# Gated cross-attention block: scores signalled by bank, and another order of the early vector and scalar work

## What is computed

```python
def reference(x, ctx, g_xattn, g_ffn, Wq, Wk, Wv, Wo, bo, w1, b1, w2, b2):
    def attention(y, context):                    # 8 heads of 64
        q, k, v = heads(y @ Wq), heads(context @ Wk), heads(context @ Wv)
        attn = softmax(einsum('bhnd,bhmd->bhnm', q, k) * 64 ** -0.5, axis=-1)
        return merge(einsum('bhnm,bhmd->bhnd', attn, v)) @ Wo + bo
    def ffn(y):                                   # 256 -> 1024 -> 256, 8-bit fixed point
        h = relu(fixed_quant(quantized_linear(y, w1, b1), 8, 4))
        return quantized_linear(h, w2, b2)
    x = x + tanh(g_xattn[0]) * attention(layernorm(x), ctx)
    return x + tanh(g_ffn[0]) * ffn(layernorm(x))
```

## Time and profile before

| | us |
|---|---|
| median of 3 runs | 120.61 |
| the runs | 119.7, 120.61, 376.62 |
| profiled execution | 120.01 |
| its span, first to last instruction | 118.2 |
| TensorE busy in the span | 111.8 (95%) |
| VectorE busy | 97.7 (83%) |
| GpSimd busy | 89.1 (75%) |
| ScalarE busy | 76.4 (65%) |

### The profile page before, as it was taken

One profiled execution on the slowest core, in us unless ns is written; L12 is line 12 of the kernel. 1 busy time (PEld: TensorE's weight loads), 2 busy tenths in 40 slices (PEclk: granted clock), 3 DMA queues, 4 the chain that ended last, 5 costly groups with the idle time before them and its releaser, 6 DMA issues.

```text
span 118.2 us, 2898 instructions
## 1 busy us (share of the span) xinstructions
PE 111.8 (95%) x1012; PEld 102.1 (86%) x1012; DVE 97.7 (83%) x223; ACT 76.4 (65%) x169; POOL 89.1 (75%) x161
## 2 busy tenths in 40 slices
PE   7979997899999999999999999999999999999990
PEld 2659976899798999988999999999999999897870
DVE  3029798999999999989999999999797979648981
ACT  4137766869688894998667575748483819448420
POOL 4003587698796989898989978996899999988720
PEclk9999999999999999999999999999999999999999
DMA  4989799300000000000010002000200020020204
GB/s 80 315 247 386 280 375 399 152 0 8 0 3 0 6 3 0 0 6 0 0 74 15 6 0 89 0 3 6 89 0 0 3 89 6 0 89 8 88 13 165
DMA packets 5328, 8.87 MB, mean 75 GB/s; under 512 B 1191, under 2 KB 2242, under 8 KB 5186
## 3 DMA queue, kind: packets, MB, share of 16 engines
q1 hardware_dynamic: 5082, 8.34, 20.1%
q10 hardware_dynamic: 232, 0.34, 0.9%
HBM read 6.59 MB, written 2.10 MB: 73 GB/s over the span
## 4 chain that ended last, share of the span: by engine, by line
PE 52%; POOL 21%; DVE 14%; DMA 5%; issue 3%; ACT 1%; SPq 1%; POOLq 0%; DVEq 0%; ACTq 0%
PE sc_ps L841 15%; PE of_ps L878 12%; PE h_ps L910 7%; DMA wq_sb<-in_L_xattn_Wq_dram 5%; POOL hid L362 5%; POOL x_sb L383 4%; PE of_ps L925 4%; POOL probs L300 4%; POOL rstd L310 3%; POOL yq L316 3%; DVE probs L614 3%; PE tr_ps L853 3%; DVE mx L609 3%; DVE den L621 2%; DVE pT L650 1%
## 5 line engine op out<-in xcount | busy, mean ns | idle before, releaser
L841 PE MATMUL sc_ps<-a_sb,xT 128*128 128x308 f32 x192 | 31.1, 311 | 0.7 <-DVE probs L614 0.7
L878 PE MATMUL of_ps<-u_sb,pT 128*128 128x256 f32 x240 | 30.9, 281 | 0.1
L878 PEld LDWEIGHTS of_ps<-u_sb,pT 128*128 128x128 f32 x240 | 29.5, 188 | 0.3 <-issue 0.3
L841 PEld LDWEIGHTS sc_ps<-a_sb,xT 128*128 128x128 f32 x192 | 27.4, 188 | 1.4 <-issue 1.2
L438 ACT ACTIVATE probs<-probs,rstd 128x616 f32<-128x616 f32 x16 | 13.1, 818 | 23.0 <-DVE probs L614 23.0
L481 ACT ACTIVATE hid_q<-h_ps,b1z 128x256 int8<-128x256 f32 x58 | 24.5, 494 | 3.6 <-PE h_ps L910 3.6
L300 POOL TENSOR_TENSOR probs<-probs,rden 128x616 f32<-128x616 f32 x16 | 19.5, 1221 | 1.9 <-DVE rden L624 1.9
L362 POOL CAST hid<-hid_q 128x512 bf16<-128x512 int8 x27 | 15.8, 611 | 2.0 <-ACT hid_q L481 2.0
L910 PE MATMUL h_ps<-x2T,w1T 128*128 128x256 bf16 x128 | 16.7, 274 | 0.0
L609 DVE TENSOR_REDUCE mx<-sc_ps 128x8 f32<-128x616 f32 x16 | 12.6, 787 | 2.8 <-PE sc_ps L841 2.7
L614 DVE TENSOR_TENSOR probs<-sc_ps,mx 128x616 f32<-128x616 f32 x16 | 12.8, 800 | 0.5
(11 more groups left out here) (124 smaller groups left out, 175.8 us busy)
## 6 DMA issues: line engine op xcount, KB each, us to landing
w_sb<-in_L_ffn_w_dram SPq DMA_DIRECT2D x2, 1024.0 KB, 10.9
out_dram<-x_sb SPq DMA_DIRECT2D x7, 256.0 KB, 2.5
x_sb<-in_x_dram SPq DMA_DIRECT2D x4, 256.0 KB, 8.0
x_sb<-in_x_dram SPq DMA_DIRECT2D x1, 1024.0 KB, 9.8
wq_sb<-in_L_xattn_Wq_dram SPq DMA_DIRECT2D x1, 512.0 KB, 5.8
wv_sb<-in_L_xattn_Wv_dram SPq DMA_DIRECT2D x1, 512.0 KB, 7.8
wo_sb<-in_L_xattn_Wo_dram SPq DMA_DIRECT2D x1, 512.0 KB, 8.6
wk_sb<-in_L_xattn_Wk_dram SPq DMA_DIRECT2D x1, 256.0 KB, 3.4
```

Source lines behind the costliest of these rows:

```text
L841: ins = nc.tensor.matmul(sc_ps[:, a, 0:HALF], xT[:, T % 2, p, c, :], a_sb[:, q, T // TB, c, HALF * a:HALF * a + HALF], start=first, stop=last)
L878: ins = nc.tensor.matmul(attn_ps, pT[:, T % 2, p, P * c:P * c + P], u_sb[:, q, MC * (T // TB) + c, :], start=first, stop=last)
```

## The change

TensorE makes the scores of bank 0 first, six matmuls, with a signal of their own, and then those of bank 1. The semaphores scores_ready, max_ready and centered count banks instead of tiles; the scores of bank a wait only for the subtraction of bank a of the tile before. center(T) takes the banks that it is to work on. Tiles 0 and 1 are centred one bank at a time, all others both at once as before. VectorE's prologue: tile 3's statistics go behind center(0), together with tile 4's; denominators(0) goes ahead of rowsT_low(2); tile 5's statistics go ahead of center(1); u_low(0, 0) goes between the two banks of center(1). In slot 0 VectorE runs probsT_low(0) ahead of denominators(1). ScalarE's prologue: exponentials(0) goes ahead of xT_copy(2), and minus_centred(3) behind it; in slot 0 pT_copy(0) and xT_copy(3) go ahead of exponentials(1). Nothing of GpSimd's or SyncE's changes.

```diff
--- before.py
+++ after.py
@@ -434,7 +434,7 @@
 
             def exponentials(T):
                 act.wait_ge(rstd1_ready, T + 1)
-                act.wait_ge(centered, T + 1)
+                act.wait_ge(centered, 2 * T + 2)
                 nc.scalar.activation(probs_v(T), probs_v(T), ACT.Exp, scale=rstd1[:, T:T + 1]).then_inc(exp_done, 1)
 
             def a_copy(n):
@@ -531,11 +531,11 @@
             act.wait_ge(v_psum, 1)
             nc.scalar.copy(values_of(0), values_psum(0)).then_inc(v01_ready, 1)
             minus_centred(2)
-            minus_centred(3)
             act.wait_ge(v_psum, 2)
             nc.scalar.copy(values_of(1), values_psum(1)).then_inc(v23_ready, 1)
+            exponentials(0)
             xT_copy(2)
-            exponentials(0)
+            minus_centred(3)
             u_copy(0, 0)
             u_copy(0, 1)
             u_copy_whole(0, 1)
@@ -545,10 +545,14 @@
             nc.scalar.activation(tg[:, :], g_sb[:, :], ACT.Tanh).then_inc(tg_ready, 1)
 
             for s in range(TILES):
+                if s == 0:
+                    pT_copy(0)
+                    xT_copy(3)
                 if live(s + 1):
                     exponentials(s + 1)
-                pT_copy(s)
-                if live(s + 3):
+                if s > 0:
+                    pT_copy(s)
+                if s > 0 and live(s + 3):
                     xT_copy(s + 3)
 
                 if s in (3, 4):
@@ -596,24 +600,33 @@
                 nc.vector.memset(pads[:, 0, 0:HEAD0], 1.0).then_inc(pad_set, 1)
 
             def stats_first(first, end):
-                dve.wait_ge(x_in[min(first, TB) // 2], 16)
                 for T in range(first, end):
+                    dve.wait_ge(x_in[min(T, TB) // 2], 16)
                     nc.vector.bn_stats(st1[:, T, :], x_sb[:, T, :]).then_inc(st1_done, 1)
                 for T in range(first, end):
                     dve.wait_ge(st1_done, T + 1)
                     nc.vector.bn_aggr(mv1[:, T, :], st1[:, T, :]).then_inc(mv1_ready, 1)
 
-            def center(T):
-                i = T % 2
-                dve.wait_ge(scores_ready, T + 1)
-                nc.vector.tensor_reduce(mx[:, i, :].rearrange("p (a h) -> p a h", a=2), sc_v, AX.X,
-                                        ALU.max).then_inc(max_ready, 1)
-                dve.wait_ge(max_ready, T + 1)
+            def maxima(T, banks):
+
+                i, h = T % 2, slice(H // 2 * banks[0], H // 2 * banks[-1] + H // 2)
+                dve.wait_ge(scores_ready, 2 * T + banks[-1] + 1)
+                nc.vector.tensor_reduce(mx[:, i, h].rearrange("p (a h) -> p a h", a=len(banks)),
+                                        sc_v[:, banks[0]:banks[-1] + 1, :, :], AX.X, ALU.max).then_inc(max_ready, len(banks))
+
+            def subtract_maxima(T, banks):
+                i, h = T % 2, slice(H // 2 * banks[0], H // 2 * banks[-1] + H // 2)
+                dve.wait_ge(max_ready, 2 * T + banks[-1] + 1)
                 if T >= 2:
                     dve.wait_ge(pT_psum, T - 1)
-                nc.vector.tensor_tensor(probs_v(T).rearrange("p (a h) m -> p a h m", a=2), sc_v,
-                                        mx[:, i, :].rearrange("p (a h) -> p a h", a=2).unsqueeze(3)
-                                        .to_broadcast([P, 2, H // 2, M]), ALU.subtract).then_inc(centered, 1)
+                nc.vector.tensor_tensor(probs_v(T)[:, h, :].rearrange("p (a h) m -> p a h m", a=len(banks)),
+                                        sc_v[:, banks[0]:banks[-1] + 1, :, :],
+                                        mx[:, i, h].rearrange("p (a h) -> p a h", a=len(banks)).unsqueeze(3)
+                                        .to_broadcast([P, len(banks), H // 2, M]), ALU.subtract).then_inc(centered, len(banks))
+
+            def center(T, banks=(0, 1)):
+                maxima(T, banks)
+                subtract_maxima(T, banks)
 
             def denominators(T):
                 i = T % 2
@@ -707,24 +720,29 @@
                                     of_ps[:, 0, :].rearrange("p (i n) -> p i n", i=2),
                                     xT[:, :, 0, :, :].rearrange("p i c n -> p i (c n)").bitcast(F32),
                                     ALU.subtract).then_inc(xT_ready, 2)
-            stats_first(2, 4)
-            center(0)
+            stats_first(2, 3)
+            center(0, (0,))
+            center(0, (1,))
+            stats_first(3, 5)
+            denominators(0)
             rowsT_low(2)
-            stats_first(4, 5)
-            denominators(0)
+            stats_first(5, 6)
+            center(1, (0,))
             u_low(0, 0)
-            center(1)
+            center(1, (1,))
             u_low(0, 2)
-            stats_first(5, 6)
             dve.wait_ge(tg_ready, 1)
 
             for s in range(TILES):
                 if live(s - 1):
                     residual(s - 1)
                     stats_second(s - 1)
+                if s == 0:
+                    probsT_low(0)
                 if live(s + 1):
                     denominators(s + 1)
-                probsT_low(s)
+                if s > 0:
+                    probsT_low(s)
                 if live(s + 3):
                     rowsT_low(s + 3)
                 if s == 4:
@@ -825,22 +843,23 @@
 
             def scores(T):
                 pe.wait_ge(xT_high, T + 1)
-                if T >= 1:
-                    pe.wait_ge(centered, T)
                 if T == TB:
                     pe.wait_ge(a1_high, DK)
                     pe.wait_ge(a1_low, DK)
-                for p, q in PARTS:
-                    if q == 1 and T == 0:
-                        pe.wait_ge(a_ready, len(a_units))
-                    if p == 1:
-                        pe.wait_ge(xT_ready, T + 1)
-                    for c in range(DK):
-                        for a in range(2):
+                for a in range(2):
+
+                    if T >= 1:
+                        pe.wait_ge(centered, 2 * T - 1 + a)
+                    for p, q in PARTS:
+                        if q == 1 and T == 0:
+                            pe.wait_ge(a_ready, len(a_units))
+                        if p == 1:
+                            pe.wait_ge(xT_ready, T + 1)
+                        for c in range(DK):
                             first, last = (c, p, q) == (0, *PARTS[0]), (c, p, q) == (DK - 1, *PARTS[-1])
                             ins = nc.tensor.matmul(sc_ps[:, a, 0:HALF], xT[:, T % 2, p, c, :],
                                                    a_sb[:, q, T // TB, c, HALF * a:HALF * a + HALF], start=first, stop=last)
-                ins.then_inc(scores_ready, 1)
+                    ins.then_inc(scores_ready, 1)
 
             def probsT(T):
                 pe.wait_ge(probs_ready, T + 1)
@@ -885,7 +904,7 @@
 
                     pe.wait_ge(x1_ready, T + 2)
                 else:
-                    pe.wait_ge(centered, TILES)
+                    pe.wait_ge(centered, 2 * TILES)
                     if T - 2 in yT_last:
                         pe.wait_ge(x2T_ready, T - 1)
                 ins = nc.tensor.transpose(yT_of(T).bitcast(BF16), yq[:, T % 2, :].bitcast(BF16), ident_b[:, :])
```

## The result

| | median, us | runs |
|---|---|---|
| before | 120.22 | 20 |
| changed | 120.53 | 20 |

The ratio of changed to before is 1.0054, with a 95% interval of 1.0031 to 1.0077: the kernel is 0.65 us slower, 0.4 to 0.9, a quarter of the 2% that would count. The ratio is taken over each kernel's fast runs alone (within 1.5% of its fastest), while the medians are of all 20, and so it says more than their distance of 0.31 us. The profiled execution of the changed kernel has a span of 118.8 us, before 118.2.

A forecast was written before the change was run, and what follows sets the result against it. VectorE was taken to bound the kernel from 19.27 to 36.24 us, then TensorE for 44 us. Bank order 0, GpSimd's queue +0.48 and the residual's slack -0.10 made +0.38 us: 120.4, own range 120.1 to 121.0, wider 119.2 to 121.3.

The forecast's parts named there:

- the step from the shift to the number: Whole kernel: a +0.38 us shift put on the profiled 120.01 us makes 120.39, likeliest value 120.4.
- From tile 2 on, VectorE does what it did: VectorE, tile 2 onward: both banks at once, after both signals, with no cost put on it.
- Tile 0 and its stall: Tile 0's scores and centring: likely stall 0.15 us, halves 0.47 us per instruction, gain 0.42 us at the subtraction.
- GpSimd's queue behind tile 3's statistics: GpSimd's prologue: late statistics delay the rstd operation, so tile 0's scaling starts about 18.90 us, 0.44 late.
- Slot 0: VectorE and ScalarE in slot 0: tile 1's denominators come 0.58 us later, second scaling at 23.61 instead of 23.03.
- They would still be 0.37 us late, because a denominator now stands behind the 0.7 us of probsT_low(0): Tile 1's denominators on VectorE: 0.37 us late even had GpSimd not been late at tile 0.
- The change does something only to what is before 36.3 us: Whole kernel: only work before 36.3 us is affected, so the question is when the transpose of 36.24 us starts.
- A shift at 36.24 us is passed on in full to the end: TensorE after 36.24 us: busy 44.00 of 44.10 us, no idle time to catch up until about 80 us.
- The banks at 0: TensorE's score matmuls: six in a row into one bank cost no more than two banks in turn, 0 us.
- Rival (a): Prologue: a gain, the 0.42 us lead of tile 0 or tile 2's scores lives on, 119.2 to 119.9 us; chance 0.27.

The follow-up runs named there:

- after_steps_of_1: The changed kernel with max_ready and centered raised by 1 where both banks are done at once (tiles 2 to 15); end 106.03 us, ratio 1.0058.
- after_both_back: The changed kernel with tile 3's statistics early, slot 0 in its old order and semaphore steps of 1; end 105.97 us, ratio 1.0056.
- before_with_halves: The kernel before with banks in turn, a signal each, and tiles 0 and 1 in halves, all else unmoved; end 105.47 us, ratio 0.9992.
- before_steps_of_2: The kernel before with max_ready and centered raised by 2 instead of 1, waits doubled; end 106.45 us, 106.41 when profiled again, ratio 1.0049.

## Why the prediction was right or wrong

That there would be a loss and the mechanism of its largest part were forecast; its size was not, and two steps of the prediction failed. The first is the step from the shift to the number. The prediction put a loss of 0.38 us on the profiled 120.01, which is +0.3%, and gave 120.4. That lies under the median of 120.61 that stood in front of me, so as a comparison of two printed numbers it had the wrong sign. The 120.61 was the middle of three runs; with 20 it became 120.22. The forecast should have been written as a difference, and as 121.0 where the median shown is the yardstick. That the median of the changed kernel, 120.53, lies 0.1 from 120.4 is luck. The second is a term put at nothing, "From tile 2 on, VectorE does what it did": the loss is 0.65 us by the timed runs and 0.77 by the traces, about twice the forecast. By the traces 0.39 us were missing: 0.11 at the transpose and 0.28 behind it, of which after_steps_of_1 gives back 0.25.

Point by point, us from the first score matmul:

| step | predicted | changed kernel |
|---|---|---|
| tile 0's subtraction ends | 3.22 | 3.16 |
| first scaling starts | 6.19 | 6.15 |
| tile 2's scores start | 7.92 | 7.87 |
| tile 1's subtraction ends | 8.62 | 8.56 |
| tile 1's reciprocal ends | 10.82 | 10.93 |
| second scaling starts | 10.90 | 11.02 |
| third scaling ends | 17.40 | 17.54 |
| transpose of tile 1's rows | 23.91 | 24.02 |
| end | 105.89 | 106.28 |

- *Tile 0 and its stall*: right. The halves took 0.48 us where 0.47 was put.
- *GpSimd's queue behind tile 3's statistics*: right, and the largest part: undoing it gives back 0.46 us.
- *Slot 0*: the term that was mis-sized by 0.11. The sum let the low part of tile 0's probabilities start 0.04 us after ScalarE's xT_copy(3) and last 0.78. ScalarE's row in the changed kernel (shown behind this list) ends at 21.52, and the low part starts at 21.65: 0.13 us, and it lasts 0.82. GpSimd's queue carried the lateness on (0.12, 0.14), and it is the 0.11 at the transpose.
- *"They would still be 0.37 us late, because a denominator now stands behind the 0.7 us of probsT_low(0)"*: the number is near (0.32 with tile 3's statistics early), the reason is not. With the denominators in front again it is 0.38 (10.61, after_both_back); with the prologue in its old order nothing is late (10.17 against 10.23 before, before_with_halves). It is the 0.43 us that the sum itself had found at tile 1's subtraction and then left, since tile 2's scores start sooner. Together, the new prologue and the new slot 0 cost 0.22 us (105.47 to 105.69).
- *"From tile 2 on, VectorE does what it did"*, and with it "The change does something only to what is before 36.3 us": the step that failed. It was costed at nothing because shapes and order are the same. The diff raises the semaphores by len(banks), which is 2, and I read that as bookkeeping. It costs VectorE 0.06 us for each tile from 2 on, and 0.25 us at the end of this kernel.
- *"A shift at 36.24 us is passed on in full to the end"*: it was passed on, but TensorE's stretch behind it wasn't as closed as its 44.00 of 44.10 us made it look. From the transpose to the end it is 81.99 us before, 82.26 changed, 82.02 with steps of 1: undoing VectorE's steps takes 0.24 of the 0.27 us away. So VectorE bounds a part of that stretch nearly together with TensorE, and a busy share of TensorE can't show how close the other is.
- *The banks at 0*: right in the steady state. The stall was in the sum for tile 0 with 0.15 us and measured 0.11; there it is masked by the gain of the halves.
- *Rival (a)* came nearest to what a repaired version does: the lead of the halves lives on once GpSimd's queue is free and VectorE's waits are filled. In the changed kernel it does not.

ScalarE's xT_copy(3) in the changed kernel:

```profile
21.14 0.38 ACT L426 CAST xT<-tr_ps 128x256 fp32r<-128x256 f32 x1
```

The ladder closes, each rung a run: 105.51 before; 105.47 with the banks in turn and the halves; + 0.50 for the prologue's new order = 105.97; - 0.28 for slot 0's new order = 105.69; + 0.34 for tile 3's statistics late = 106.03; + 0.25 for the steps of 2 = 106.28. In another order the rungs have other sizes, as the 0.46 for tile 3's statistics shows.

## What to carry to other kernels

When work is moved back on one engine, list every queue in which something waits for it, and add up what stands behind that wait, however small: a statistics operation that GpSimd reads moved the scaling of tile 0, and with it three slots. A new order is worth nothing as long as the waits that it opens are not filled (0.68 us for tile 1's exponential, 0.49 for tile 0's, enough for a pair of instructions). Raise a semaphore by 1 in each instruction of a tight dependent pair, and let the waiter count in other numbers instead.

## What the runs showed of the hardware

- An instruction that raises a semaphore by 2 has its wait in an instruction ahead of it; the gap between two dependent VectorE instructions is then 0.09 us instead of 0.03, and the count of instructions rises (2898 to 2916) or falls when it is undone (2915 to 2901). The trace of before had such a wait already, at L705.
- VectorE paused about 0.38 us more than elsewhere at one instruction, 0.5 us after the last of the copies that it waits for had ended, in three executions of two programs. The cause is open.
- Two profiled executions of one kernel agree within 0.04 us (before) and 0.05 us (before_steps_of_2) from the first score matmul on, while that matmul itself moved between 11.6 and 13.9 us over the runs. A stretch of a trace tells 0.1 us where twelve timed runs tell 0.3.
